# Four decaying-sum units computed beside expert tiles, homes behind the turnings, one activation set in a scan loop, two layout queues

## The reference

```python
def _birwkv(r, k, v, w, u):
    ew = jnp.exp(wc); ek = jnp.exp(k)
    Af, Bf = _wkv_scan(ek, v, ew)                      # carry before token t: A = ew*A + ek*v, B = ew*B + ek
    Ab, Bb = _wkv_scan(ek[:, ::-1], v[:, ::-1], ew)    # the same from the end
    cur = jnp.exp(uc + k)
    wkv = (Af + Ab + cur * v) / (Bf + Bb + cur)
    return jax.nn.sigmoid(r) * wkv
```

## Time and profile before

| what | value |
|---|---|
| time, median of 3 runs | 2384.69 us (2382.84 to 2394.42) |
| the profiled execution | 2390.27 us, span 2388.5 us |
| PE busy | 2038.9 us (85%) |
| DVE busy | 1441.8 us (60%) |
| ACT busy | 938.4 us (39%) |
| POOL busy | 783.7 us (33%) |
| mean granted clock of PE | 0.935 of full speed |

### The profile page before, as it was taken

One profiled execution on the slowest core, in us unless ns is written; L12 is line 12 of the kernel. 1 busy time (PEld: TensorE's weight loads), 2 busy tenths in 40 slices (PEclk: granted clock), 3 DMA queues, 4 the chain that ended last, 5 costly groups with the idle time before them and its releaser, 6 DMA issues. The chain is left out here.

```text
span 2388.5 us, 37231 instructions
## 1 busy us (share of the span) xinstructions
PE 2038.9 (85%) x14090; PEld 1438.0 (60%) x14107; DVE 1441.8 (60%) x2869; ACT 938.4 (39%) x1590; POOL 783.7 (33%) x555
## 2 busy tenths in 40 slices
PE   6998857983995786599878889998999989899998
PEld 5775544662985675599535655783443434455887
DVE  3886875576323566211374554235799999999333
ACT  3434423430111343133334431113775756655443
POOL 1221231234002201100313014005688798977200
PEclk9999988996997886799988999999999999999999
DMA  5217010003994100799100003482210101200000
GB/s 169 81 41 265 24 42 31 2 19 135 349 396 153 52 20 18 273 357 381 53 1 28 2 2 136 131 260 84 80 45 27 41 31 39 82 9 1 10 9 18
DMA packets 104721, 232.65 MB, mean 97 GB/s; under 512 B 10016, under 2 KB 77472, under 8 KB 95584
## 3 DMA queue, kind: packets, MB, share of 16 engines
q1 hardware_dynamic: 95808, 208.24, 24.7%
q0 software_dynamic: 7680, 20.98, 2.7%
q10 hardware_dynamic: 1056, 1.05, 0.1%
HBM read 174.27 MB, written 55.97 MB: 96 GB/s over the span
## 5 line engine op out<-in xcount | busy, mean ns | idle before, releaser
L4295 POOL TENSOR_TENSOR l_attn_ring<-l_attn_ring,l_attn_c_rows 128x1024 f32<-128x1024 f32 x128 | 301.4, 2355 | 76.8 <-DVE l_attn_ring L4107 76.8
L4107 DVE TENSOR_TENSOR_SCAN l_attn_ring<-bank,l_attn_ring 128x512 f32<-128x512 f32 x256 | 299.1, 1210 | 21.6 <-ACT bank L3911 17.0
L3667 PE MATMUL bank<-l_attn_ring,identity 128*128 128x512 f32 x512 | 245.8, 602 | 17.0 <-POOL l_attn_ring L4295 13.7
L3911 ACT ACTIVATE bank<-l_attn_step,l_attn_minus_exp_a_log 128x508 f32<-128x508 f32 x256 | 173.7, 685 | 156.2 <-DVE l_attn_ring L4107 155.8
L170 PE MATMUL bank<-x_features,weights 128*128 128x512 f32 x416 | 204.5, 627 | 17.0 <-ACT l_attn_silu_z L3825 4.9
L3667 PEld LDWEIGHTS bank<-l_attn_ring,identity 128*128 128x128 f32 x512 | 95.5, 192 | 124.3 <-issue 97.3
L4101 DVE TENSOR_TENSOR l_attn_ring<-l_attn_step_times_input,bank 128x1024 f32<-128x1024 f32 x128 | 153.2, 1197 | 1.8 <-issue 1.3
L598 DVE TENSOR_REDUCE negmax_slots<-bank 128x16 f32<-128x2048 f32 x48 | 109.8, 2287 | 59.6 <-PE bank L467 59.1
L170 PEld LDWEIGHTS bank<-x_features,weights 128*128 128x128 f32 x416 | 79.0, 199 | 106.7 <-issue 86.1
L179 PE MATMUL bank<-weights,x_features 128*128 128x256 f32 (+1 forms) x336 | 101.6, 457 | 7.2 <-ACT weights L3941 2.4
L578 ACT ACTIVATE l_xattn_probs<-bank 128x1024 f32<-128x1024 f32 x64 | 62.1, 1021 | 97.9 <-PE bank L467 97.9
(11 more groups left out here) (750 smaller groups left out, 4434.3 us busy)
## 6 DMA issues: line engine op xcount, KB each, us to landing
l_attn_tile_weights<-l_ffn_experts SPq DMA_DIRECT2D x22, 2180.0 KB, 10.0
ffn_experts_tile_weights<-l_ffn_experts_experts SPq DMA_DIRECT2D x37, 1024.0 KB, 8.2
expert_slots<-zeros SPq DMA_DIRECT2D x8, 2048.0 KB, 11.7
l_attn_c_rows<-state_outputs SPq DMA_DIRECT2D x64, 256.0 KB, 3.2
l_ffn_tile_weights<-l_ffn_experts SPq DMA_DIRECT2D x23, 512.0 KB, 4.4
expert_slots<-residual_sum SPq DMA_DIRECT2D x62, 128.0 KB, 8.1
expert_slots<-zeros SPq DMA_DIRECT2D x1, 5888.0 KB, 27.5
l_ffn_tile_x<-expert_slots SPq DMA_DIRECT2D x23, 256.0 KB, 4.2
```

The source lines that it names most:

```text
L3667: mm = pe.matmul(net.banks[SUMS[j]][:], net.ident[:], ring[n % 4][:, j, :], start=s == 0, stop=s == STATES - 1)
L3911: nc.scalar.activation(by_seq(net.banks[DECAY[j]][:])[:, :, 1:], by_seq(dt[:, m, :])[:, :, 1:], ACT.Exp, scale=a[:, m * STATES + s:m * STA ...
L4107: nc.vector.tensor_tensor_scan(ring[n % 4][:, j, :], net.banks[DECAY[j]][:], ring[n % 4][:, j, :], 0.0, ALU.mult, ALU.add).then_inc(state_ ...
L4295: tt(ring[n % 4][:], ring[n % 4][:], c_row[:, n % STATES, :].unsqueeze(1).broadcast_to([P, 2, T]), ALU.mult).then_inc(out_ready, 1)
```

## The change

1. `l0_xattn` no longer computes units 4 to 7. A new class, `LateWkv`, computes them in `l0_ffn_experts`: ACT's exponentials ahead of its table load, POOL's products, eight pieces per unit on DVE (one per tile from tile 1 on, between taking the turned tile t + 2 and copying the result of t), SP's stores behind tiles 10, 18, 26 and 34. The stage's parameters grow by 524 columns.
2. `l0_xattn` stores the last group as two pairs, and `load_across` issues the even transfers from SP and the odd ones from ACT.
3. `Homes` runs behind the first turnings and hidden products: DVE after `take_xT(1)`, PE between `turn(2)` and `out(0)`.
4. `Sparse.run_sp` reads the row numbers of the tiles whose rows were loaded ahead behind the first loads, not ahead of them.
5. The scan loop loads a set that holds logarithm and exponential (`preload_act_table_set`) once ahead of the loop and again behind each silu and root, in place of the loads for each function.

```diff
+class LateWkv:
+    PIECES = 8
...
+    def exp_act(self, act, w):
+        nc = self.net.nc
+        act.wait_ge(self.net.ready["l0_ffn_experts"], 16)
+        nc.scalar.activation(self.decay, w["w"], ACT.Exp).then_inc(self.consts_ready, 1)
+        nc.scalar.activation(self.bonus, w["u"], ACT.Exp).then_inc(self.consts_ready, 1)
+        for at, n in enumerate(self.units):
+            nc.scalar.activation(self.ek(at)[:, :, 1:P + 1], self.values(n), ACT.Exp).then_inc(self.ek_ready, 1)
...
+    def piece_dve(self, dve, chain, p):
...
+        if i == 0:
+            dve.wait_ge(self.ekv_ready, at + 1)
+        if i < 4:
+            self.scan(n, ek if i % 2 else self.ekv, i, i >= 2)
+        elif i == 4:
+            dve.wait_ge(self.scanned, 4 * (at + 1))
+            for k, own in enumerate((self.ekv, ek)):
+                total = self.scans[k][:, :, 0:P]
+                chain.step(nc.vector.scalar_tensor_tensor(out=total, in0=own[:, :, 1:P + 1],
+                                                          scalar=self.bonus[:, f:f + 1], in1=total,
+                                                          op0=ALU.mult, op1=ALU.add))
+        elif i == 5:
+            chain.settle()
+            nc.vector.engine_nop().then_inc(self.used, 1)
+            for k in range(2):
+                total = self.scans[k][:, :, 0:P]
+                chain.step(nc.vector.tensor_tensor(total, total, self.scans[2 + k][:, :, 2:P + 2], ALU.add))
+        elif i == 6:
+            chain.settle()
+            chain.step(nc.vector.reciprocal(self.scans[1][:, 0:2, 0:P], self.scans[1][:, 0:2, 0:P]))
+        else:
+            chain(nc.vector.reciprocal(self.scans[1][:, 2:NB, 0:P], self.scans[1][:, 2:NB, 0:P]))
+            dve.wait_ge(self.net.wkv_stored, 16 * n)
+            nc.vector.tensor_tensor(self.by_seq(self.out), self.scans[0][:, :, 0:P], self.scans[1][:, :, 0:P],
+                                    ALU.mult).then_inc(self.out_ready, 1)
+            dve.wait_ge(self.out_ready, at + 1)
...
                 def store(g):
-                    sp.wait_ge(x_ready, NB * (g + 1))
-                    net.store_group(sp, g)
+                    if g < GROUPS - 1:
+                        sp.wait_ge(x_ready, NB * (g + 1))
+                        net.store_group(sp, g)
+                        return
+                    for n in range(last, SEQUENCES, 2):
+                        sp.wait_ge(x_ready, n + 2)
+                        net.store_pair(sp, n)
...
-                wkv.exp_act(act, 0)
...
-                    wkv.pieces_dve(dve, chain, k)
...
-                wkv.product_pool(pool, n)
...
                 load_table(net, ACT.Exp)
+                net.load_across(act, 1)
...
-        load_x(0)
+        if not self.rows_ahead:
+            load_x(0)
         for t in range(1, early):
+            if t >= len(self.rows_ahead):
+                load_x(t)
+            load_w(t)
+        for t in range(len(self.rows_ahead)):
             load_x(t)
-            load_w(t)
...
+            if t == 0 and before_out:
+                before_out()
             out(t)
...
         take_xT(1)
+        if behind_first:
+            behind_first()
         for t in range(self.tiles):
             if t + 2 < self.tiles:
                 take_xT(t + 2)
+            if between:
+                between(t)
             dve.wait_ge(self.out_in_psum, t + 1)
...
-                homes.bring_pe(pe, BROUGHT, spread_ready, brought)
-                pe.wait_ge(dve_steps, 8)
-                experts.run_pe(pe)
+                def numbers_home():
+                    homes.bring_pe(pe, BROUGHT, spread_ready, brought)
+                    pe.wait_ge(home, 1)
+                experts.run_pe(pe, numbers_home)
...
+                late.exp_act(act, w)
                 load_table(net, ACT.Gelu)
...
-                load_table(net, ACT.Exp)
+                logarithms_and_exponentials()
...
-                load_table(net, ACT.Ln, 1.0)
                 logarithm(0, 0, 2)
...
                     if at == 1 and g >= 1:
                         silu_z(g - 1)
+                        logarithms_and_exponentials()
                     if at == 13 and g + 1 < GROUPS:
                         silu_u(g + 1)
+                        logarithms_and_exponentials()
...
                         root_of_context(0)
+                        logarithms_and_exponentials()
...
+        def load_across(queue, first):
+            queue.wait_ge(x_stored[0], 16 * (GROUPS - 1 + NB // 2))
+            for n in range(first, SEQUENCES, 2):
+                queue.dma_start(net.x_all[:, n, :], across_rows(between[0], n)).then_inc(net.x_back[0][n // NB], 16)
```

More of the change, by code:

```diff
@@ L1202, in take @@
                     return heads.take_slots(heads.qT[g % 2], src, ACT.Relu, i, w["own"])
-                def rest(k):
-                    if k:
-                        wkv.exp_act(act, k)
-                heads.run_act(act, take, rest)
+                heads.run_act(act, take)
             @block.vector
@@ L1903, in run_act, with run_dve @@
                 ins.then_inc(self.hidden_ready, 1)
-    def run_dve(self, dve):
+    def run_dve(self, dve, behind_first=None, between=None):
         net, nc = self.net, self.net.nc
@@ L2036, in l0_ffn_experts @@
         homes, route = Homes(net), net.routing
+        late = LateWkv(net, net.scratch(sub), net.signals(48)[41:], range(FIRST_UNITS, Wkv.UNITS))
         BROUGHT = net.banks[experts.OUT[0]]
@@ L2040, in l0_ffn_experts, with at_tile, do @@
         beside[18], beside[24] = prefetch, net.load_groups
+        stores = {late.PIECES * (at + 1) + 2: at for at in range(len(late.units))}
+        def at_tile(t):
+            def do(sp):
+                if t in beside:
+                    beside[t](sp)
+                if t in stores:
+                    late.store_sp(sp, stores[t])
+            return do
         with nc.Block() as block:
@@ L2044, in _ @@
             def _(sp):
-                experts.run_sp(sp, beside)
+                experts.run_sp(sp, {t: at_tile(t) for t in [*beside, *stores]})
                 experts.wait_stored(sp)
+                sp.wait_ge(net.wkv_stored, 16 * Wkv.UNITS)
             @block.tensor
             def _(pe):
-                homes.bring_pe(pe, BROUGHT, spread_ready, brought)
-                pe.wait_ge(dve_steps, 8)
-                experts.run_pe(pe)
+                def numbers_home():
+                    homes.bring_pe(pe, BROUGHT, spread_ready, brought)
+                    pe.wait_ge(home, 1)
+                experts.run_pe(pe, numbers_home)
             @block.scalar
             def _(act):
+                late.exp_act(act, w)
                 load_table(net, ACT.Gelu)
@@ L2061, in _, with numbers_home, between @@
                 chain = Chain(dve, dve_steps)
-                homes.spread_dve(chain, [a[:] for a in route.slot + route.weight], spread_ready)
-                homes.take_dve(dve, chain, BROUGHT, brought)
-                nc.vector.engine_nop().then_inc(dve_steps, 1)
-                experts.run_dve(dve)
+                def numbers_home():
+                    homes.spread_dve(chain, [a[:] for a in route.slot + route.weight], spread_ready)
+                    homes.take_dve(dve, chain, BROUGHT, brought)
+                    nc.vector.engine_nop().then_inc(home, 1)
+                def between(t):
+                    if t == 0:
+                        late.consts_dve(dve, chain, w)
+                    else:
+                        late.piece_dve(dve, chain, t - 1)
+                experts.run_dve(dve, numbers_home, between)
+            @block.gpsimd
+            def _(pool):
+                late.run_pool(pool)
     net.homes = homes
@@ L4469, in store_group, with store_pair @@
             sp.dma_start(group_rows(between[0], g), net.x_all[:, g * NB:(g + 1) * NB, :]).then_inc(x_stored[0], 16)
[L4471 to L4474 removed]
+        def store_pair(sp, n):
+            sp.dma_start(between[0][n:n + 2].rearrange("b t d -> t b d"),
+                         net.x_all[:, n:n + 2, :]).then_inc(x_stored[0], 16)
+        def load_across(queue, first):
+            queue.wait_ge(x_stored[0], 16 * (GROUPS - 1 + NB // 2))
+            for n in range(first, SEQUENCES, 2):
+                queue.dma_start(net.x_all[:, n, :], across_rows(between[0], n)).then_inc(net.x_back[0][n // NB], 16)
         def store_across(sp, g):
```

80 lines of the change are left out of this document (66 added, 14 removed).

## The result

The changed kernel takes 2361.03 us (median of 6 runs, 2357.11 to 2375.05) against 2390.48 us of the kernel before in the same comparison (6 runs, 2382.84 to 2396.68): ratio 0.9882, 95% interval 0.9857 to 0.9908. The forecast was 2364.8 us. The profiled execution took 2371.86 us, span 2370.1, which is 18.4 us less than the profiled execution before; the forecast for that difference was 19.9.

What follows compares the result with a forecast made beforehand. No single bound: PE and DVE nearly level in the cross-attention, PE and DMA in the expert stage, DVE in the scan loop. -9.5 + 0.5 - 1.7 - 0.7 - 8.5 = -19.9 us from 2384.69 gave 2364.8 us; range 2354 to 2380.

Steps and rivals of the forecast that it cites:

- rival D: Cross-attention, border and scan loop gain more than the sum: -28.2 us in all, 2356.5 us; chance 0.14.
- Part 1: First cross-attention: decaying sums leave DVE, most of PE's 10.8 us waits for the maximum go; -9.5 us, ends 0 and -14.
- the 1 beside it: Cross-attention, last four sequences: a shorter DVE queue also shortens the step between waits; 1 us added to the 8.5.
- The end of -14: Cross-attention's largest gain: all 10.8 us of waits, plus 3.2 more.
- Rival A: The cross-attention keeps its length because PE then waits for ACT or the shift; 2374.3 us, chance 0.18.
- Part 2: Expert stage takes the sums: +0.5 us from DVE delaying tiles, +1.0 from the stores' bandwidth.
- Part 3: Expert stage, token homes behind the turnings: the wait between homes and turning is saved; -1.0 us, ends -1.5 and +1.
- Part 4: Border at 353 us: two issuing queues -1.2, smaller last store -0.5; -1.7 us, ends 0 and -3.
- Part 5: Layer-1 experts: second tile's weights requested before two register reads; -0.7 us, ends 0 and -1.45.
- Part 6: Scan loop, one table set: DVE's waits for ACT's table loads go; -8.5 us, ends -11 and -4.
- rival B: Scan loop: preloads don't replace the table loads but come on top; +9 instead of -8.5, 2382.3 us, chance 0.10.
- +1.0 of its 1.28: Scan loop: one preload comes ahead of the copy PE waits for, costing 1.0 us of its 1.28.

Runs made afterwards that it cites:

- e5: The changed kernel once more, unedited, beside the kernel before: 2368.57 us, ratio 0.991 to the kernel before.
- e7: The changed kernel with two pieces of the sums per tile on tiles 1 to 16, stores behind tiles 6, 10, 14 and 18: 2371.29 us, ratio 0.9926.
- e3: The kernel before with only the border's pairs and two queues, homes behind the turnings, and row numbers behind the first loads: 2384.35 us, ratio 0.9977.
- e6: The changed kernel without the four stores of the late quotients and the waits for them: 2361.29 us, ratio 0.9884.
- e1: The kernel before with only the four sum units moved from the first cross-attention into the expert stage: 2382.86 us, ratio 0.9962.
- e8: The changed kernel with all sixteen border loads issued by SP on one queue, pairs kept: 2362.48 us, ratio 0.989.
- e4: The changed kernel with the scan loop's table-set preload put behind the copies for the previous unit: 2362.7 us, ratio 0.9867.
- e2: The kernel before with only the one table set in the scan loop: 2381.79 us, ratio 0.9969.
- e10: The changed kernel with the copies for the previous unit ahead of silu and the table-set preload in the scan loop: 2361.08 us, ratio 0.9888.
- e9: The changed kernel with each piece of the sums behind the copy of the tile's result instead of ahead: 2366.57 us, ratio 0.9896.

## Why the prediction was right, and where its terms were not

The time came out 3.8 us under the forecast, and no rival took its place. But part of that closeness is luck. The forecast was worked from a median of 2384.69 us for the kernel before; in the comparison that median is 2390.48, so the gain measured there is 29.45 us, not 19.9. As a share it is 1.18%, and 0.9% in e5, against a forecast of 0.83%. By the first of these alone rival D, with its 28.2 us, would fit as well; the stages decide against it, as none of the three parts that D enlarged (1, 4 and 6) reached the size it gave them. And the sum is right partly because terms that were too small stand beside terms that were too large.

- **Part 1, -9.5: right in the mechanism, mis-sized.** From the first to the last L533 it took 128.15 us before, and 115.82 or 115.83 in every kernel without the sums there but one: -12.3 (e7: 115.84). The windows over that stretch, before and after, with the columns of the earlier trace rows:

```profile
210.41:338.56 128.15, 104.19 (x1671) 72.73 (x1672) 113.32 (x157) 54.29 (x70) 37.24 (x26) 0.97 0.29 97
```

```profile
215.67:331.50 115.83, 100.82 (x1673) 70.62 (x1672) 67.71 (x119) 52.70 (x67) 21.00 (x23) 1.00 0.28 96
```

PE's idle time fell from 24.0 to 15.0 us, by 9.0: the waits for the maximum fell by 10.2, and 1.3 came back elsewhere, mostly as longer waits for ACT. That is close to the 8.5 of the sum, which let a fifth come back. What was sized too small is the 1 beside it: PE's busy time fell by 3.4 us. Behind two of the six waits (2.47 and 2.02 us) PE's next products of L467 had run at a granted clock of 0.50 to 0.55, 2.09 and 1.95 us instead of 1.17; that went too. The end of -14 held. The stage itself is 10.4 us shorter in the profiled pair, mostly because its first eight products, where nothing is edited, ran at a granted clock of 0.70 instead of 1.00 in the execution after (5.24 us instead of 3.67). Rival A falls: what came back is a small part of what went.
- **Part 2, +0.5 and +1.0: the size nearly held, the reason didn't.** The sums cost 2.4 us (e3 to after; 0.3 to 3.7 over the profiles with the same code). DVE doesn't hold PE up at a tile's taking in beyond the 0.4 us at the start, and the waits for tile rows grew by 0.3 to 2.2 us, but they are as long without the stores (e6). The additions, two of 0.78 in the sum, took 0.69 and, in three of four units, 1.67. With the homes still first, the sums cost 7.4 us (e1). That interaction wasn't in my sum, which added parts 2 and 3 as if each stood alone.
- **Part 3, -1.0: mis-sized.** The first output is 9.18 us behind the barrier instead of 11.36, -2.2 (-1.7 to -2.5 in the nine kernels with this order). The removed wait is what I counted; what I missed is the bringing of the homes itself. It takes 0.96 us at a granted clock of 1.00 where it took 1.89 at 0.50: PE now comes to it from other products, and came to it from a pause of 19.69. PE's work at the start of the stage in the kernel after:

```profile
578.55 1.09 PE L1947 MATMUL bank<-identity,ctx_tokens 128*128 128x128 f32 x4 [18.29 <-PEq L132]
580.03 5.24 PE L170 MATMUL bank<-l_ffn_experts_tile_xT,x_features 128*128 128x128 f32 x32 [0.40 <-DVE l_ffn_experts_tile_xT L2021]
...
585.33 0.96 PE L2119 MATMUL bank<-ctx_tokens 128*128 128x16 f32 x8
587.08 1.99 PE L179 MATMUL bank<-x_features,l_ffn_experts_hidden 128*128 128x256 f32 x8 [0.79 <-DVEq L2188]
```

- **Part 4, -1.7: this step failed.** Its term for the two queues, "With two queues the first four are issued in 1.3 instead of 2.5 us: -1.2", measures less than 0.1, the difference of the means under e8. The fourth issue did start 0.85 us sooner, but DVE waits for the arrival of the loads, not for their issue. (ACT's eight issues took 6.1 us instead of the 5 of the sum; they end 0.2 us behind the start of the first statistics.) The sign that I gave, first statistics under 6 us behind the first issue, came true by chance: 5.89 in the profile after, 6.06 to 6.75 in the seven others with two queues. The term of the pairs is right: from the barrier to the first issue 1.95 before, 1.29 to 1.32 after, -0.6 (forecast -0.5). (The stage as a whole is no measure of it: it takes 232.1 to 234.9 us in the nine kernels with the pairs, 233.9 to 235.6 in the three without.) The Trainium skill, "DMA: Bandwidth & Descriptors", section "Issuing engines are not separate DMA queues", says that several engines' transfers share the same 16 DMA engines and that only issuing time is saved. The trace agrees: 4 us of issuing were saved, and the wait is 5.9 to 6.8 us with two queues and 6.2 to 6.4 with one. By that rule the term was 0.5, and the rule was the better forecast.
- **Part 5, -0.7: outside its ends.** The second tile's weights are asked for 1.25 us behind the barrier instead of 2.42, as counted. But the stage is 3.0 us shorter. PE's products for tile 1 start 10.43 us behind the barrier instead of 11.75 (-1.3), and their 32 products took 3.81 us (granted clock 1.00) in six kernels with the new order and 5.44 (0.69) in three, against 5.44 to 6.76 in the three with the old. The sum had no term for the products. The pause ahead of them is 1.18 to 3.68 us with the new order, 3.16 to 4.92 with the old. What puts the products at 3.81 isn't the length of the pause alone: 3.81 stands behind a pause of 3.02 in e3, 5.44 behind one of 2.33 in e4. Pause and products in the kernel after, on PE's timeline:

```profile
978.13 3.81 PE L170 MATMUL bank<-l_attn_tile_xT,l_attn_tile_weights 128*128 128x128 f32 x32 [1.46 <-DMA l_attn_tile_weights<-l_ffn_experts]
```

- **Part 6, -8.5: the loop's gain was right, its loss too small.** The table loads of the loop's region went from 27 to 17 (rival B falls), and DVE's work came earlier by 1.6 us at the loop's head and by 1.2, 2.0, 2.2 and 2.2 at its four logarithms, 9.1 together, forecast 9.5. The step that failed is "+1.0 of its 1.28". At the preload ahead of the copy 3.1 us were lost (4.4 in e2): 1.4 of pause, and the rest behind slower products. At the last unit 5.6 us of the lead are left. Then 1.6 us were lost behind the loop in a spell of some 3.4 us at half clock, at 2183.8 us in the kernel after. It is there in after, e3, e4, e5, e6, e8 and e10 and not in before, e1, e2, e7 and e9; nothing in these runs says what brings it. Layer 3 is 4.0 us shorter, 5.6 in e2.

By stages of the profiled pair that makes -10.4 (part 1), +0.6 (2 and 3), -1.8 (4), -3.0 (5), -4.0 (6) = -18.6, against terms of -9.5, +0.5, -1.7, -0.7 and -8.5. The stages without edits moved by +0.8, +2.9, -0.1 and -3.5 and cancel.

## What to carry to other kernels

Before an instruction is moved ahead of another on a half-idle engine, ask whether a busy TensorE waits for the second one: here the pause cost its own length and then, in slower products, about as much again (1.42 of pause and 1.0 to 1.8 behind it), and where a pause was removed, slower products went with it (9.0 of idle time and 3.4 of busy time in the cross-attention). Work moved beside a stage that another engine bounds was nearly free here while each piece stayed under what a tile leaves (2.58 us): DVE got 46 us more to do, and the stage grew by 0.3 to 3.7. At twice the rate it grew by 8 us, mostly because two of the four results then waited 3.0 and 3.8 us for the store of the one before, so check the buffers as well as the lengths. What comes first in that stage decides as much as the piece does. The second issuing queue shortened the issuing and not the arrival, so price it by the time from the first issue to the first landed load.

## What the runs showed of the hardware that was not expected

The same four products, behind the same pause of 1.93 us for the same copy, took 1.98 us at a granted clock of 1.00 in three kernels and 3.09 at 0.62 in a fourth; so what a pause costs in the products behind it isn't fixed by its length, and only a range can be forecast. And a stage without any edit took from 217.7 to 230 us between kernels, with the granted clock from 0.78 to 0.72 and DVE's busy time constant at 138 us: a gain of half a per cent on this kernel can be seen in the lengths of a stage over several kernels but not in one run's total.

DVE's work was longer beside POOL's. The second addition of a unit takes 1.67 us in the three units in which POOL's product of the next unit runs at that time (610.67 to 612.15 for the first), and 0.69 in the fourth, in which POOL has nothing to do. No run takes POOL's product away, so that the one slows the other is read from the times alone.
